# An attention and MXFP8 feed-forward kernel: one low half moved to VectorE, query weights sent apart, and the engines' hand-written orders replaced

## What is computed

```python
def _mx_dequant(t):                      # blocks of 32 along the last dim
    scales = jnp.maximum(max_abs / 448.0, 1e-30)
    q = (blocks / scales[..., None]).astype(jnp.float8_e4m3fn).astype(jnp.float32)
    return (q * scales[..., None]).reshape(rows, feat)

query, key = ctx @ Wq.T + bq, ctx @ Wk.T + bk
attention = softmax(query @ key.T, axis=-1)
x = x + layernorm(x) @ attention.T                     # per batch, 512 x 512
y = layernorm(x)
h = silu(mx(y) @ mx(gate_w).T) * (mx(y) @ mx(up_w).T)   # 2048 wide
x = x + mx(h) @ mx(down_w).T
```

## Time and profile before

| | us |
|---|---|
| median of 3 runs | 611.02 |
| the profiled execution | 610.0 |
| its span, first to last instruction | 608.0 |
| PE busy | 600.6 (99%) |
| DVE busy | 484.0 (80%) |
| ACT busy | 309.2 (51%) |
| POOL busy | 44.8 (7%) |
| granted TensorE clock, mean | 0.999 |

### The profile page before, as it was taken

One profiled execution on the slowest core, in us unless ns is written; L12 is line 12 of the kernel. 1 busy time (PEld: TensorE's weight loads), 2 busy tenths in 40 slices (PEclk: granted clock), 3 DMA queues, 4 the chain that ended last, 5 costly groups with the idle time before them and its releaser, 6 DMA issues.

```text
span 608.0 us, 7215 instructions
## 1 busy us (share of the span) xinstructions
PE 600.6 (99%) x2683; PEld 282.3 (46%) x2683; DVE 484.0 (80%) x455; ACT 309.2 (51%) x463; POOL 44.8 (7%) x60
## 2 busy tenths in 40 slices
PE   8999999999999999999999999999999999999998
PEld 3456554444444444444444444444444444444446
DVE  4999998899999999988999985131148899989740
ACT  3999989553555555853475532431121515254520
POOL 0000002100000001010110201000000000001100
PEclk9999999999999999999999999999999999999999
DMA  8989869989988978867445655750010334557691
GB/s 314 396 206 275 234 177 256 280 193 249 208 207 209 219 159 210 174 140 171 124 112 97 148 112 113 165 86 0 1 19 0 53 69 83 90 105 101 110 171 35
DMA packets 148162, 92.28 MB, mean 152 GB/s; under 512 B 134304, under 2 KB 134688, under 8 KB 143264
## 3 DMA queue, kind: packets, MB, share of 16 engines
q1 hardware_dynamic: 142656, 63.78, 45.2%
q0 software_dynamic: 5472, 28.05, 19.9%
HBM read 25.76 MB, written 8.39 MB: 56 GB/s over the span
## 4 chain that ended last, share of the span: by engine, by line
PE 85%; DMA 5%; issue 3%; ACT 3%; DVE 1%; SPq 1%; POOL 0%; DVEq 0%; ACTq 0%
PE bank L727 49%; PE bank L739 17%; PE bank L742 9%; PE bank L711 5%; DMA h<-in_ctxT 2%; PE bank L702 1%; PE bank L695 1%; DMA xT<-hT 1%; PE bank L687 1%; PE bank L757 1%; DMA W<-hT 1%; DMA h<-hT 1%; ACT hT L944 1%; PE bank L762 1%; ACT h L987 0%
## 5 line engine op out<-in xcount | busy, mean ns | idle before, releaser
L727 PE MATMUL bank<-gu_hi,xT 128*128 128x512 f16 x1024 | 243.6, 380 | 1.7 <-DMA xT<-hT 1.7
L727 PEld LDWEIGHTS bank<-gu_hi,xT 128*128 128x128 f16 x1024 | 99.9, 98 | 123.4 <-DMA xT<-hT 3.2
L727 PE MATMUL bank<-gu_lo,xT 128*128 128x512 f16 x512 | 131.5, 379 | 0.0
L739 PE MATMUL bank<-dn,hT 128*128 128x512 f16 x480 | 106.1, 379 | 0.0
L1633 DVE SCALAR_TENSOR_TENSOR h<-bank,unscale,silu 128x512 f32<-128x512 f32 x64 | 47.4, 747 | 56.1 <-PE bank L727 36.1
L1088 ACT ACTIVATE silu<-bank,unscale 128x512 f32<-128x512 f32 x64 | 42.8, 679 | 83.4 <-PE bank L727 40.3
L727 PEld LDWEIGHTS bank<-gu_lo,xT 128*128 128x128 f16 x512 | 50.1, 98 | 60.4
L739 PEld LDWEIGHTS bank<-dn,hT 128*128 128x128 f16 x480 | 47.0, 98 | 56.6
L1114 ACT ACTIVATE W<-h 128x2048 f16<-128x2048 f32 x16 | 30.5, 1909 | 68.3 <-DVE W L1665 25.4
L711 PE MATMUL bank<-dn,h 128*128 128x512 f32 x128 | 55.9, 593 | 0.0
L742 PE MATMUL bank<-dn,hT 128*128 128x512 f16 x240 | 54.3, 379 | 0.0
(11 more groups left out here) (119 smaller groups left out, 560.1 us busy)
## 6 DMA issues: line engine op xcount, KB each, us to landing
W<-hT POOLq DMA_DIRECT2D x12, 1024.0 KB, 5.9
W<-in_units SPq DMA_DIRECT2D x11, 1024.0 KB, 5.7
h<-W POOLq DMA_DIRECT2D x7, 1024.0 KB, 6.1
h<-in_xcols SPq DMA_DIRECT2D x4, 1024.0 KB, 12.6
out_y<-y POOLq DMA_DIRECT2D x12, 256.0 KB, 6.2
h<-in_xrows SPq DMA_DIRECT2D x2, 1024.0 KB, 11.8
out_y<-h SPq DMA_DIRECT2D x2, 1024.0 KB, 5.5
h<-hT POOLq DMA_DIRECT2D x2, 1024.0 KB, 5.9
```

The lines of the kernel that those rows point to most:

```text
L727: last = pe.matmul(bank[:, :], xT[:, b % 2, part, k, :], w[:, c, g, j * 512:(j + 1) * 512], start=(j == 0 and not low), stop=(j == HT - 1 ...
L739: pe.matmul(bank[:, :], hT[:, r % 2, 0, k, :], dn[:, w, k, :], start=(k == 0 and w == 0), stop=False)
```

## The change

- rows_by_vector is (0,): the low part of row batch 0 is made by DVE from the high part; rows_rest(0) on POOL and rows_lo(0) on ACT are gone, and SP's wait for them.
- The 256 columns of query weights come in a transfer of their own. At the start SP now issues: slice, the other 386 constant columns, the query weights, context 0, the rest of u0 in two, context 1, u1, contexts 2 and 3, x rows 0, x columns 0, x rows 1, x rows 2, u2, x columns 1. ACT and the second projection wait for both parts of the constants; the first projection waits for a count of 16 and its context.
- keep_zeros runs 10 matmuls and not 11.
- The orders of SP, POOL, PE, ACT and DVE and bank_uses are replaced throughout.

The diff, cut to its core (bank_uses, most of ACT's list and exchanges of neighbours in the later lists left out). The settings and the loads:

```diff
     units_by_vector = ()
-    rows_by_vector = ()
+    rows_by_vector = (0,)
+    apart = True
...
+            def load_query_weights():
+                sp.dma_start(late[:, 1024:1024 + 256], consts[:, 0:256]).then_inc(consts_in, 16)
             def load_consts():
-                sp.dma_start(late[:, 1024:1538 + P], consts).then_inc(consts_in, 16)
+                first = 256 if apart else 0
+                sp.dma_start(late[:, 1024 + first:1538 + P], consts[:, first:]).then_inc(consts_in, 16)
```

SyncE:

```diff
             load_slice(0)
+            load_consts()
+            load_query_weights()
             load_ctx(0)
-            load_consts()
             load_half(0)
             load_rest(0)
-            load_rows(0)
             load_ctx(1)
             load_unit(1)
+            load_ctx(2)
             load_ctx(3)
-            load_ctx(2)
+            load_rows(0)
+            load_columns(0)
             load_rows(1)
+            load_rows(2)
             load_unit(2)
-            load_columns(0)
-            load_rows(2)
             load_columns(1)
             sp.wait_ge(*unit_rest_in(0))
             turn_unit_hi(0)
+            load_rows(3)
             load_unit(3)
+            load_columns(2)
+            sp.wait_ge(*unit_rest_in(1))
             turn_unit_lo(0)
-            load_rows(3)
+            turn_unit_hi(1)
             store_rows(0)
-            sp.wait_ge(*unit_rest_in(1))
-            turn_unit_hi(1)
-            load_columns(2)
+            turn_unit_lo(1)
             load_unit(4)
-            turn_unit_lo(1)
+            load_columns(3)
+            sp.wait_ge(*unit_rest_in(2))
             turn_unit_hi(2)
-            load_columns(3)
-            sp.wait_ge(*rows_rest_in(0))
             turn_rows_hi(0)
             turn_rows_lo(0)
             store_rows(1)
             turn_unit_lo(2)
             load_unit(5)
-            store_rows(2)
             sp.wait_ge(*unit_rest_in(3))
             turn_unit_hi(3)
             turn_unit_lo(3)
             load_unit(6)
+            store_rows(2)
             store_rows(3)
             sp.wait_ge(*unit_rest_in(4))
             turn_rows_hi(1)
...
+            turn_rows_hi(3)
+            sp.wait_ge(*hidden_rest_in(5))
+            turn_rows_lo(3)
             turn_hidden_hi(5)
```

GpSimd:

```diff
-            pool.wait_ge(wT_in[1], 16)
+            pool.wait_ge(wT_in[0], 16)
             unit_rest(1)
...
-            rows_rest(0)
```

TensorE:

```diff
+                if b == 0 and i == 1 and apart:
+                    pe.wait_ge(consts_in, 32)
...
-            keep_zeros(11)
+            keep_zeros(10)
             pe.wait_ge(consts_in, 16)
             project(0, 0)
             project(0, 1)
             energies(0, 0)
+            project(1, 0)
             energies(0, 1)
+            project(1, 1)
             energies(0, 2)
             energies(0, 3)
-            project(1, 0)
-            project(1, 1)
...
             product(3, 0)
             product(1, 0)
+            turn_probs(3, 3)
             product(0, 0)
+            product(2, 0)
             attend(3, 0)
             attend(3, 1)
             attend(3, 2)
             attend(3, 3)
-            product(2, 0)
             product(3, 1)
             product(2, 1)
             product(6, 0)
...
             down(2)
             product(11, 0)
+            down(3)
             product(11, 1)
             product(11, 2)
-            down(3)
             down(4)
```

VectorE:

```diff
             add_attended(1, 2)
             add_attended(1, 3)
+            rows_lo(0)
+            attended_means(1)
             unit_reduce(4)
-            attended_means(1)
             add_attended(2, 0)
-            unit_power(3)
-            add_attended(2, 1)
-            add_attended(2, 2)
             unit_round(3)
             unit_largest(4)
             unit_dequant(3)
-            unit_power(4)
+            hidden_of(3, 0)
             rows_scale(1)
             unit_scale(4)
-            add_attended(2, 3)
             rows_round(1)
             rows_dequant(1)
+            unit_power(4)
+            add_attended(2, 1)
             unit_round(4)
-            hidden_of(3, 0)
+            add_attended(2, 2)
+            add_attended(2, 3)
             unit_dequant(4)
             unit_reduce(5)
             add_attended(3, 0)
             add_attended(3, 1)
             unit_largest(5)
             add_attended(3, 2)
+            hidden_of(1, 0)
             add_attended(3, 3)
-            hidden_of(1, 0)
```

More of the change, by code:

```diff
@@ L657, in _ @@
             add_out(1)
+            second_norm(3)
             rows_rest(3)
+            pool.wait_ge(nT_in[0], 64)
+            hidden_rest(5)
             add_out(2)
-            pool.wait_ge(nT_in[1], 64)
-            hidden_rest(5)
             add_out(3)
+            pool.wait_ge(hT_in[0], 112)
             hidden_rest(6)
@@ L804, in _ @@
             attend(0, 1)
+            energies(2, 3)
+            turn_probs(1, 0)
+            energies(3, 0)
             attend(0, 2)
-            energies(2, 3)
+            turn_probs(1, 1)
+            energies(3, 1)
             attend(0, 3)
-            turn_probs(1, 0)
-            turn_probs(1, 1)
             turn_probs(1, 2)
@@ L812, in _ @@
             turn_probs(2, 0)
-            energies(3, 0)
-            energies(3, 1)
+            turn_probs(2, 1)
+            energies(3, 2)
             attend(1, 0)
+            energies(3, 3)
             attend(1, 1)
-            turn_probs(2, 1)
             attend(1, 2)
@@ L821, in _ @@
             turn_probs(2, 3)
-            energies(3, 2)
-            energies(3, 3)
+            turn_probs(3, 0)
+            turn_probs(3, 1)
             attend(2, 0)
@@ L901, in _ @@
             product(11, 3)
-            down(6)
             product(15, 0)
             product(15, 1)
+            down(6)
+            product(15, 2)
             down(7)
             down(8)
-            product(15, 2)
             down(9)
@@ L1231, in _ @@
-            unit_lo(2)
-            silu_of(3, 0)
-            take_probs(3, 0)
+            unit_magnitude(3)
+            row_variances(3, 1)
+            take_probs(3, 0)
+            unit_lo(2)
+            center_by_scalar(1, 0)
+            silu_of(3, 0)
+            center_by_scalar(1, 1)
+            take_probs(3, 1)
+            take_probs(3, 2)
+            weigh(3, 3)
+            unit_hi(3)
             attended_variances(1, 0)
-            unit_hi(3)
-            take_probs(3, 1)
             attended_variances(1, 1)
-            take_probs(3, 2)
+            silu_of(1, 0)
@@ L1337, in _ @@
-            hidden_magnitude(4)
-            center_by_scalar(3, 1)
-            attended_variances(3, 0)
-            hidden_hi(3)
-            silu_of(9, 0)
+            hidden_rescale(2)
+            hidden_magnitude(2)
+            hidden_hi(2)
+            center_by_scalar(3, 0)
+            hidden_unscale(1)
+            silu_of(8, 0)
+            hidden_rescale(3)
+            silu_of(8, 1)
+            hidden_unscale(2)
+            hidden_magnitude(3)
+            center_by_scalar(3, 1)
@@ L1351, in _ @@
+            silu_of(9, 3)
+            rows_hi(3)
+            hidden_magnitude(5)
             silu_of(10, 0)
[L1352 to L1365 removed]
@@ L1366, in _ @@
-            hidden_rescale(7)
-            hidden_hi(6)
-            silu_of(11, 2)
+            hidden_lo(4)
+            take_down(2)
+            hidden_magnitude(6)
+            hidden_rescale(5)
+            hidden_rescale(6)
+            hidden_hi(5)
+            rows_lo(3)
+            silu_of(11, 0)
+            hidden_lo(5)
+            hidden_unscale(3)
+            silu_of(11, 1)
+            hidden_unscale(4)
+            hidden_magnitude(7)
+            hidden_rescale(7)
+            hidden_unscale(5)
@@ L1771, in _ @@
             unit_round(6)
+            hidden_of(2, 1)
             unit_reduce(7)
-            hidden_of(2, 1)
+            hidden_of(6, 0)
+            hidden_of(6, 1)
             unit_largest(7)
@@ L1777, in _ @@
             unit_dequant(6)
-            hidden_of(6, 0)
+            unit_power(7)
             unit_round(7)
-            hidden_of(6, 1)
             unit_reduce(8)
```

494 lines of the change are left out of this document (232 added, 262 removed).

## The result

The changed kernel takes **615.99 us** (median of 5 runs, 613.82 to 618.16) where the kernel before, run beside it, takes 610.43 (609.1 to 611.29): ratio 1.0100, 95% interval 1.0081 to 1.0119. It is slower by 5.6 us; I had said 609.0 and a range up to 612.2. The profiled execution took 613.82 (span 612.0), 3.8 more than that of before.

A forecast was written before the change was run, and what follows sets the result against it. PE bounds the kernel, so only early holes could be gained: +0.1 - 0.95 + 0.3 - 1.1 - 0.65 - 0.3 (crumbs) + 0.6 = -2.0 us, giving 609.0 us against the 611.0 median; 8-in-10 range 607.4 to 612.2.

The forecast's parts named there:

- What bounds the kernel: Whole kernel: PE is busy 600.6 of 608.0 us; only early holes can be gained, 3.5 us at most.
- After 140 ... I count 0: Behind 140 us: neighbours swap order, no operation is added and PE did not wait there, so no change in time.
- ACT has room: Behind 140 us: ACT's spare capacity, given as one reason for counting 0 there.
- The start, "+0.1": First projection: starts at 5.95 us, when the context lands fourth, against 5.87 before; bounds 5.45 to 6.3.
- rival 3: First two projections: PE's clock rises later, +0.4 us (609.4), at worst +2.9 (611.9); chance 0.05.
- The third context, -0.95: Third context, near 18 us: lands about 4 us sooner, so the 0.95 us wait for it goes.
- Batch 0's low half, -1.1 and -0.65: Near 92 us: with DVE making the low half, waits for both turned halves go, 1.1 and 0.65 us.
- ACT's lateness, +0.3: Ahead of product(3,0): ACT ends take_probs(2,3) at 75, where PE wants it 0.2 to 0.3 us sooner.
- Batch 1, +0.6: product(6,0): turned half lands at 136.6 us, a wait of 1.1 where 0.5 stood.
- Rivals 1 and 4: 1: attend(3,3)-to-batch-1 chain keeps length, 613.5 us, chance 0.15; 4: SP chain or ACT late at 92 us, 610.7, chance 0.08.
- rival 2: Batch 1 at product(6,0): DVE or DMA late, landing between 137.4 and 139.8, returns the whole gain, about 611 us; chance 0.22.
- the stall behind 140 "that I did not find": Behind 140 us: an unidentified stall of no stated size, sharing with rival 1 the 0.18 chance of slower.

The follow-up runs named there:

- e2: Changed kernel with hidden_hi(10) moved ahead of hidden_magnitude(13) in ACT's list; 612.05 us, ratio 1.0028.
- e3: Changed kernel with e2's edit on ACT and e1's edit on DVE together; 611.72 us, ratio 1.0028.
- f1: e3 with the old order of first loads (context 0 ahead of all constants in one transfer), ten zeros kept; 608.38 us, ratio 0.9975.
- f4: Kernel before with only the changed start: slice, other constants, query weights, context 0, and ten zeros; 613.48 us, ratio 1.0054.
- e1: Changed kernel with hidden_dequant(12) and hidden_of(15, 2) moved between hidden_lo(10) and hidden_lo(11) on DVE; 616.1 us, ratio 1.0099.
- e4: Changed kernel with 13 filling matmuls, their sums overwritten, put ahead of down(14); 615.21 us, ratio 1.0091.
- f3: e3 with 24 zero matmuls in place of ten; 610.73 us, ratio 1.0013.
- g1: f1 with batch 0's low half made by ACT again, not by DVE, with POOL's adding transfer and SP's wait back; 612.46 us, ratio 1.0047.
- g2: f1 with SyncE's store_rows(3) moved behind the turnings of batch 1; 607.08 us, ratio 0.9966.
- g4: Changed kernel with hidden_scale(15) and hidden_lo(13) moved behind hidden_dequant(14) on DVE, hidden_magnitude(15) behind hidden_hi(14) on ACT; 621.13 us, ratio 1.0193.
- g6: Changed kernel with DVE's hidden_scale(15) behind hidden_dequant(14), hidden_lo(14) right after it, and ACT's hidden_magnitude(15) behind hidden_hi(14); 615.98 us, ratio 1.0112.
- f2: e3 with first loads in the order slice, query weights, context 0, other constants; 609.03 us, ratio 0.9982.
- g5: g2 with add_attended(2,2) also moved ahead of unit_round(4) on DVE; 606.68 us, ratio 0.9951.

## Why the prediction was wrong, by its steps

- **What bounds the kernel: right** in that holes ahead of 140 us are all that can be gained. "It can only lose" behind it was right too, and I priced the loss at nothing.
- **"After 140 ... I count 0": this step failed**, and is 4.4 us (e2). I took PE's not waiting for slack. It is none: the rows that were wanted were the distance from each turned half's landing to the matmul that wants it. I worked two such margins (down(3), product(12,0)), both in the pieces that moved far, and none at the end, where pieces moved by a few places. ACT began h14's high half at 575.72 for a matmul at 584.07; it was turned from 577.65 to 582.75, which left 1.3 us. "ACT has room" (50% busy) is a mean, and so is DVE's 80%: what counts is who waits behind whom. hidden_magnitude(13) waits 8.69 us for DVE with hidden_hi(10) queued behind it, for which DVE waits.
- **The start, "+0.1": failed in size**, 3.2 us (e3 to f1) or 3.3 (f4). I took "the same bytes at the same rate"; the landing is 6.96 to 8.42, beyond my upper bound of 6.3. The bound was "one issue later"; what two small transfers ahead do to a large one was in no row, and I should have left the upper end open. Then the clock: rival 3, with 0.05, came true in f4, e1 and e4, but by a hole of 2.5 us or more and not of 0.5, and by half in e2 and e3. There I had the mechanism and gave it the wrong chance, since it hung on the landing. By the Trainium skill ("TensorE: Matmul & The Clock Gate", Part 1) the throttled state is the default, and activity releases it. The rows agree: 24 zeros without a wait (f3) are followed by fast projections, and ten zeros with a wait of 2.5 us by slow ones (f4). With ten zeros the full level was first granted at anything from 3.8 us (e4) to 13.7 us (f4), so a single trace doesn't tell what this start costs.
- **The third context, -0.95: right.** No wait is left there.
- **Batch 0's low half, -1.1 and -0.65: right.** Product(3,0) has no wait. The walk said 78.7 us from first energies to product(3,0), and it is 90.28 - 11.55 = 78.7. ACT's lateness, +0.3, didn't come. g1 shows that DVE's instruction is what does it.
- **Batch 1, +0.6: right within 0.4.** Predicted 136.6 with a wait of 1.1; it is 137.51, of which 0.85 comes from the start, with a wait of 0.75. Part of that is luck: the store was issued at 128.24, 0.9 us later than forecast beyond the start's 0.85, and the turned half landed 9.2 us behind it and not 10.1. The 0.67 us ahead of attend(3,2), a bank that add_attended(2,2) frees behind unit_round(4), I had as "0.7 us to spare". The store I named as what holds the turning: it landed at 134.61, the turned half at 137.47, and g2 bears it out.
- **The sum.** For the first 140 us I said -2.0, with 0.1 of it for the start; f1, which has the new front without the new start, gives -1.5 (0.9975). Front -1.5, start +3.2 and tail +4.4 make +6.1 us; 1.0% is measured, 5.6 to 6.1. With 1.4 us of uncertainty on the two large terms, so close a sum is partly luck.
- **Rivals.** Rivals 1 and 4 didn't occur; the landing of 137.47 is at the near edge of rival 2's, by as much as the start was late, and product(6,0) kept a gain of 1.06 us. What did occur is the stall behind 140 "that I did not find", and a part of 0.18 was too little for 470 us in which the lists were rewritten.

## What to carry to other kernels

A stage in which the bounding engine never waits isn't a stage with slack. Where hand-written orders change, take the margin of every hand-over there (landing to first use), the last ones first, since nothing behind them can win time back. On an engine that serves two others, ask of each wait in its list what stands behind it. And when a small transfer is put ahead of a large one that the first matmul needs, don't price it by its bytes alone: a trace of the new order is the only thing here that gave its cost.

## What the runs showed of the hardware

- A hole of 2.7 to 2.8 us in an otherwise full stream of 512-column matmuls (down(14) in the changed kernel and e1, product(3,0) in g1) was followed each time by matmuls at 0.43 us, at a granted clock of 0.55 to 0.60 in the changed kernel's and g1's stretches; one of 0.9 us (product(6,0) in f1) by none. g4's hole of 3.1 us and g6's of 2.2 us, both among half-width matmuls at the end, weren't either. Between these sizes no run tells.
- At the start, behind ten zeros, holes of 1.5 us (changed kernel) and 2.2 us (g4) were followed by projections at full pace, those of 2.1 to 2.7 us in e2, e3 and g6 by some four slow matmuls, and those of 2.5 to 3.5 us in f4, e1 and e4 by six or seven. The length of the hole alone doesn't decide it.
- The same context transfer took 3.7 to 4.2 us to land as the second issued (before, f1), 3.4 us as the third behind 128 KB of constants (f2), and 4.85 to 6.3 as the fourth behind two constant transfers of 321 KB together, and its landing then scattered by 1.5 us over nine traces.
- A transposing transfer's own issue (batch 1's high half) took 1.78 us on SyncE's free queue (g2, g5) and 3.1 to 4.9 us in the other 14 traces, with a 1 MB store in flight ahead of it.
- In every trace the 100 or so transfers of SyncE's queue landed in the order in which they were issued, the transposing ones too.
